# Retention block on one core: when group two's x is quantized for the linear branch, and how the first projection starts

## The reference

```python
xn = _layernorm(x, axis=-1)
# branch 1: retention
q = heads((x @ Wq + bq) * scaling); k = heads(x @ Wk + bk); v = heads(x @ Wv + bv)
ret = einsum('bhid,bhjd->bhij', q, k) * D        # D: causal, decays with distance
ret = ret / clip(abs(ret.sum(-1)), 1.0)
attn = einsum('bhij,bhjd->bhid', ret, v)
g = group norm of attn per head, times gn_w, plus gn_b
out1 = (silu(x @ Wg + bg) * g) @ Wo + bo
# branch 2: linear layer on values rounded to a 4-bit grid in blocks of 16
xq, xs, _ = quantize_nvfp4(x2d, x_tensor_scale)
wq, ws, _ = quantize_nvfp4(weight)
out2 = einsum('mbk,nbk->mn', xq * xs, wq * ws) * output_scale + bias
x = x + out1 + out2
```

## Time and profile before

| | |
|---|---|
| median of three runs | 2097.94 us (2096.73 to 2098.29) |
| the profiled execution | 2103.1 us, its span 2101.3 us |
| PE busy | 2025.2 us, 96% of the span |
| DVE busy | 1643.7 us, 78% |
| ACT / POOL busy | 692.0 us / 888.0 us |
| mean granted TensorE clock | 0.991 of 2.4 GHz |
| DMA | 297.95 MB, mean 142 GB/s |

### The profile page before, as it was taken

One profiled execution on the slowest core, in us unless ns is written; L12 is line 12 of the kernel. 1 busy time (PEld: TensorE's weight loads), 2 busy tenths in 40 slices (PEclk: granted clock), 3 DMA queues, 4 the chain that ended last, 5 costly groups with the idle time before them and its releaser, 6 DMA issues.

```text
span 2101.3 us, 53238 instructions
## 1 busy us (share of the span) xinstructions
PE 2025.2 (96%) x18894; PEld 1118.2 (53%) x18894; DVE 1643.7 (78%) x4375; ACT 692.0 (33%) x1359; POOL 888.0 (42%) x634
## 2 busy tenths in 40 slices
PE   4998989999999999999999999999999999999999
PEld 2444455555555555555555555555555555555544
DVE  7899898889989887777766778777777777777832
ACT  5656532222323232232333233233223233323310
POOL 1233333324333325555434555544554554455530
PEclk8999999999999999999999999999999999999999
DMA  8878643343543434444343355344445435435543
GB/s 309 281 254 283 221 141 101 110 119 101 141 130 109 130 98 118 130 140 122 103 132 115 114 145 141 101 124 125 108 128 142 132 96 140 109 107 145 153 157 116
DMA packets 268714, 297.95 MB, mean 142 GB/s; under 512 B 204224, under 2 KB 204352, under 8 KB 268352
## 3 DMA queue, kind: packets, MB, share of 16 engines
q1 hardware_dynamic: 268624, 296.78, 47.1%
HBM read 205.23 MB, written 41.42 MB: 117 GB/s over the span
## 4 chain that ended last, share of the span: by engine, by line
PE 58%; DVE 33%; issue 5%; DMA 2%; ACT 1%; DVEq 0%; POOL 0%; SPq 0%; POOLq 0%
PE mm L1494 27%; PE mm L1511 9%; PE mm L1422 6%; PE tp L1422 6%; PE mm L1431 3%; DVE state L1239 2%; DVE xa L1032 2%; DVE xa L1031 2%; PE four L1569 2%; DVE xa L1039 2%; DVE gst L1253 2%; PE four L1582 2%; DVE xa L1038 2%; DVE xm L1034 1%; DVE probs L1012 1%
## 5 line engine op out<-in xcount | busy, mean ns | idle before, releaser
L1494 PE MATMUL mm<-xnT,wring 128*128 128x512 f16 x4800 | 1076.6, 382 | 20.0 <-ACT kT L815 9.4
L1494 PEld LDWEIGHTS mm<-xnT,wring 128*128 128x128 f16 x4800 | 462.9, 98 | 562.5 <-issue 24.8
L1511 PE MATMUL mm<-wring,xnT 128*128 128x256 f16 x2688 | 302.8, 273 | 2.4 <-DVE res L1371 2.0
L877 ACT ACTIVATE work<-four,gs 128x64 f32<-128x64 f32 x512 | 158.1, 414 | 399.2 <-DVE gs L1266 399.2
L1511 PEld LDWEIGHTS mm<-wring,xnT 128*128 128x128 f16 x2688 | 261.3, 98 | 47.7 <-DVE res L1371 11.2
L643 POOL TENSOR_TENSOR yT<-gn,gate 128x512 f32 (+1 forms) x64 | 89.6, 1400 | 368.0 <-ACT gn L888 244.9
L1422 PE MATMUL mm<-wo,yT 128*128 128x512 f16 x960 | 215.8, 382 | 2.8 <-POOL yT L648 2.2
L1253 DVE BATCH_NORM_STATS2 gst<-four 128x6 f32<-128x64 f32 x512 | 73.5, 217 | 152.2 <-PE four L1582 151.3
L620 POOL TENSOR_TENSOR qparts<-qT,qparts 128x512 f16<-128x512 f32 x64 | 78.3, 1223 | 254.6 <-ACT qT L815 254.6
L656 POOL TENSOR_TENSOR nparts<-work,nparts 128x512 f16<-128x512 f32 x41 | 47.4, 1156 | 265.1 <-ACT nparts L863 265.1
L1422 PEld LDWEIGHTS mm<-wo,yT 128*128 (+1 forms) x960 | 91.3, 98 | 112.2 <-issue 3.4
(11 more groups left out here) (209 smaller groups left out, 2970.1 us busy)
## 6 DMA issues: line engine op xcount, KB each, us to landing
wring<-parts SPq DMA_DIRECT2D x252, 512.0 KB, 4.2
xt<-in_x SPq DMA_DIRECT2D x34, 512.0 KB, 4.6
out<-res SPq DMA_DIRECT2D x32, 512.0 KB, 3.0
parts<-wo SPq DMA_DIRECT2D x28, 512.0 KB, 5.8
res<-in_x SPq DMA_DIRECT2D x28, 512.0 KB, 3.6
ftile<-in_w_f SPq DMA_DIRECT2D x12, 512.0 KB, 4.9
parts<-wring SPq DMA_DIRECT2D x8, 512.0 KB, 6.9
probs<-in_x SPq DMA_DIRECT2D x5, 512.0 KB, 4.9
```

Of the source, the lines that this page charges most:

```text
L877: last = nc.scalar.activation(work[:, c * P + h * HD:c * P + (h + 1) * HD], ao[h][:, c * VW:c * VW + HD], ACT.Identity, bias=gs[:, 1, g:g ...
L1494: last = MM(mm[n % 2][:], wring[:, slot, wj, k, :], xnT[:, parity, xj, k, :], start=(j == 0), stop=(j == 3 * KT - 1))
L1511: last = MM(out[:, c], xnT[:, parity, xj, k, tokens], wring[:, 1::2, wj, k, :], start=(n == 0), stop=(n == 3 * KT - 1))
```

## The change

It has three parts.

**Quantization moved.** In group one VectorE no longer quantizes. SP stores the normalised rows to a DRAM tensor `xn1` (`keep_xn`), as eight units of 128x512, and the transposes of `xq` and the 1 MB copy to `xq1` are gone. In the eight bodies of groups four and five (the first two of MIDDLE) VectorE does one unit each with 16 instructions in three places: `unit_scales` behind `states(0)`, `unit_grid` behind `mask_scores(1)`, `unit_round` behind the first `emit_linear`. SP adds four DMAs in such a body: the load of the unit, its transpose within SBUF, the store to `xq1`, and in front of this a wait for the transpose, all ahead of `move_n(1)` and of the next body's loads.

**First projection in three passes.** `project_first` does the eight hi·hi matmuls when `hi_done` 1 is there, then hi·lo of x, then lo·hi when `lo_done` 1 is there. The banks that the first transposes of x use are permuted, so that mm0 and mm1 come free early.

**ScalarE's and GpSimd's order at the start.** The evacuation of mm0 comes before `split_hi` of slices 4 and 5, that of mm1 before slices 6 and 7. GpSimd's bias addition waits for `lo_done` 5.

```diff
-        x_banks = [four[:, 2], four[:, 3], four[:, 0], four[:, 1], tp[0], tp[1], mm[0], mm[1]]
+        x_banks = [four[:, 2], mm[0], mm[1], four[:, 3], four[:, 0], four[:, 1], tp[0], tp[1]]
...
+def takes_unit(phase, group):
+
+    return phase == MIDDLE and group < 3 + UNITS // CH
...
+                def keep_xn():
+
+                    w("xn_ready", 1)
+                    sp.dma_start(a["xn1"][2 * i:2 * i + 2].rearrange("h p e -> p h e"),
+                                 xt[:].rearrange("p (h e) -> p h e", h=2)).then_inc(s["xn_kept"], 16)
+
+                def load_unit():
+
+                    w("u_ready", 0)
+                    sp.dma_start(ftile[:, 0:GROUP], a["xn1"][ds(i, 1)].rearrange("a p e -> p (a e)"))\
+                      .then_inc(s["u_loaded"], 16)
+
+                def turn_unit():
+
+                    w("u_ready", 1)
+                    sp.sem_inc(sp_turn, 1)
+                    sp.dma_start(xqf[:, GROUP:].rearrange("p (k t) -> p k t", t=P), xqf[:, 0:GROUP], transpose=True)\
+                      .then_inc(s["u_turned"], 16)
+
+                def keep_unit():
+
+                    w("u_turned", 1)
+                    sp.dma_start(a["xq1"][:, ds(i * GROUP, GROUP)], xqf[:, GROUP:]).then_inc(s["u_kept"], 16)
...
                     load_slice(0, 1)
+                    keep_xn()
                     load_fs(F_TILES[i][0])
...
-                    w("xq_ready", 1)
-                    move_x()
+                    w("xn_kept", 1)
                     load_x(1)
...
+                if takes_unit(phase, group):
+                    load_unit()
                 load_slice(0, 0)
...
+                if takes_unit(phase, group):
+                    turn_unit()
                 move_x()
+                if takes_unit(phase, group):
+                    keep_unit()
                 move_n(1)
...
-                if phase == SECOND:
-                    sp.wait_ge(s["xq_moved"], at("xq_moved", SECOND, 0, 0))
-                    sp.dma_start(a["xq1"], xqT[:, 1].rearrange("p c k t -> p (c k t)")).then_inc(xq1_kept, 16)
...
             pool.wait_ge(bias_in, 16 * 2)
+            pool.wait_ge(lo_done, HK + 1)
...
             split_hi(0, range(0, 4))
             square(0, range(4, SLICES))
-            split_hi(0, range(4, SLICES))
...
                 evacuate(0, 0)
+                if i == 0:
+                    split_hi(0, range(4, 6))
                 evacuate(0, 1)
+                if i == 0:
+                    split_hi(0, range(6, SLICES))
...
+                def unit_scales():
+
+                    w("u_loaded", 1)
+                    quantize_scales(ftile[:, 0:GROUP], x_ts, x_r6, late_qs)
+                    w("u_turned", 0)
+
+                def unit_grid():
+                    find_grid(ftile[:, 0:GROUP], late_qs[:, 4, :])
+
+                def unit_round():
+                    round_to_grid(xqf[:, 0:GROUP], late_qs[:, 3, :]).then_inc(s["u_ready"], 1)
...
                     layernorm(xt[:])
-                    w("xn_ready", 1)
-                    quantize_scales(xt, x_ts, x_r6)
-                    w("xq_moved", 0)
-                    quantize_half(xt, 0)
-                    if i:
-                        quantize_half(xt, 1)
                     mask_scores(0)
-                    if i == 0:
-                        quantize_half(xt, 1)
...
                 states(0)
+                if takes_unit(phase, group):
+                    late_part(unit_scales)
                 group_norm(0)
                 mask_scores(1)
                 if phase in QUANTIZE:
                     f_half(0)
+                if takes_unit(phase, group):
+                    late_part(unit_grid)
                 states(1)
                 emit_half(w, 0, "mm0", 5)
                 if phase == MIDDLE:
                     emit_linear(w, 0, "mm1", 5, "mm0", 5)
+                    if takes_unit(phase, group):
+                        late_part(unit_round)
...
+                def project_first():
+
+                    pe.wait_ge(s["xnT_ready"], CH)
+                    pe.wait_ge(s["xhi_ready"], 2 * CH)
+                    pe.wait_ge(hi_done, 1)
+                    for wj, xj in ((0, 0), (0, 1), (1, 0)):
+                        if xj:
+                            pe.wait_ge(s["xnT_ready"], 2 * CH)
+                        if wj:
+                            pe.wait_ge(lo_done, 1)
+                        for k in range(KT):
+                            last = MM(mm[0][:], wring[:, 0, wj, k, :], xnT[:, 0, xj, k, :],
+                                      start=(k + xj + wj == 0), stop=(wj == 1 and k == KT - 1))
+                    last.then_inc(s["mm0_full"], 1)
```

60 lines of the change are left out of this document (42 added, 18 removed).

## The result

The changed kernel takes 2091.42 us in the median of eight executions (2086.01 to 2092.78), the kernel before 2098.11 (2093.90 to 2101.34, eight): a ratio of 0.9965, interval 0.9954 to 0.9977. That is 6.7 us faster, where 19.1 were forecast; 2091.4 lies 1.4 us above the range. The direction was right, the size was not.

A forecast was written before the change was run, and what follows sets the result against it. VectorE's quantization was taken to delay TensorE in group one, TensorE's own work to bound from group four. 6.7 + 3.9 + 4.1 + 5.9 - 1.5 = 19.1 us off the 2097.9 median gave 2079 us, range 2071 to 2090.

The forecast's parts named there:

- 1.7 us of slow clock: Group one's first body: third projection was to lose its 2.41 us wait and 1.7 us of slow clock.
- DMA included: Group one: 1.5 us taken back for one more VectorE wait on a weight tile, DMA share 0.93 in 55 us.
- Part 1, the first body: Start and first body of group one: earlier first projection and VectorE chain, gain 6.7 us (ends 3.5 and 8.8).
- 3 to 4 us for that slice: First body: the reloaded slice that ScalarE's last square of the second batch needs comes 3 to 4 us sooner.
- Part 2, bodies two to four: Group one: masks no longer wait behind quantization, state increments follow the projection; gains 3.9, 4.1 and 5.9 us.
- the rival that had the rings hold group one: DMA rings hold group one: gain only 8 to 12 us, time 2088 us, chance 0.2.
- Part 3, the units: Groups four and five: eight bodies with VectorE's 16 added instructions and SP's DMAs, costed at 0.
- 10.4 us of VectorE's waits: Groups four and five: VectorE's three waits for TensorE per body, 2.75, 3.61 and 4.07 us, taken to cover the units.
- the slack of the masks: Groups four and five: masks behind group norm have 2.8 us until TensorE needs them.
- if GpSimd stretches all of them: Groups four and five: with all unit instructions stretched, 11 us against 10.4 of waits, costing 0.6 us a body.
- My own sign of being wrong: Forecast is wrong if TensorE idles in bodies with a unit; it was to stay at 99.8% in groups four and five.
- The rival that was to come out slower: Groups four and five: SP's wait for its own transpose delays move_n(1) and weights; 2103 us, chance 0.05.

The follow-up runs named there:

- no_units: Changed kernel without loading, computing or storing units; xq1 filled with group three's values by one DMA: 2084.12 us, ratio 0.9937 to the kernel before.
- the second profile of before: Kernel before, unchanged, run and traced once more: median 2099.43 us, profiled execution 2099.24 us at a clock of 0.993.
- units_dma_only: Changed kernel keeping all four DMAs of a unit, VectorE's 16 instructions replaced by one copy of two columns: 2086.17 us, ratio 0.9934 to the kernel before.
- start_only: Kernel before with only the changed kernel's start (three passes, evacuation order, held-back bias addition, permuted banks), quantization left in group one: 2096.57 us, ratio 0.9992.
- units_early: Changed kernel with unit_round directly behind unit_grid, both ahead of the second states: 2088.86 us, ratio 0.9949 to the kernel before.
- the repetition: Changed kernel, word for word, run again beside the kernel before: 2090.72 us, ratio 0.9967.

## Why the prediction was wrong

**The sum was made on one execution, and fitted it partly by luck.** I wrote that the 19.1 us come off the profiled execution and subtracted them from the median. `no_units`, the changed kernel without the part that I costed at nothing, has a span of 2080.6, 20.7 under the 2101.3 of before; my 19.1 was 1.6 off. But its terms miss in both directions: the first body gave 4.3 us less than I took (2.4 for 6.7), and the rest of group one and the first body of group two 4.2 more (16.6 for 12.4, DMA included).

The terms also held stretches at 1.2 GHz of one execution as if they were the kernel's: the 8.08 of the earlier trace rows, "1.7 us of slow clock" of the third projection, the 2.00 of the earlier trace rows, the 6.45 of the earlier trace rows. Against the second profile of before the trace of `no_units` is 16.8 ahead, and where the changed code meets such stretches itself (`units_dma_only`) it loses up to 4 us to them. In medians the change without units gives 13.5 us (2097.65 to 2084.12), not 19.1. The profiled executions account for the distance between 20.7 and 13.5: that of before stood 5.4 us over its median, at a clock of 0.991 where the mean of 26 executions is 0.994, and that of `no_units` 1.8 under its own, at 0.998 where three of the five have 0.996. I had noted that the profiled execution stood 5.2 us over the median and drew nothing from it, and I took for granted that the changed kernel would run without any.

**Part 1, the first body: mis-sized.** I took 6.7 us. The first pass came at 24.77 (forecast 25.0), the three passes ended at 30.66 (32.5 to 33), the layer norm started at 43.32 (42.4 to 43.4): the start is as I described it, and the lead at the first scores 9.2. The step that failed is "3 to 4 us for that slice": ScalarE's last square came 0.8 us earlier than in the earlier trace rows, and TensorE, which waits for it, met a lower clock behind the wait, so the second body began with 2.4 us in the profiles. Without the store of xn (`start_only`) the square came 2.4 us earlier and the second body began with 5.3. In medians the runs show 1.1 us for this part alone and 0.3 on top of the move. I had seen the full queue and the store of xn ahead of the reload, and then followed VectorE's rows and not the slice's.

**Part 2, bodies two to four: right.** Leads grew by 4.4, 3.1 and 6.1 us where I had 3.9, 4.1 and 5.9. Body lengths of 55, an undisturbed projection at the fourth body, and masks beside TensorE's projection are there. Against the second profile of before they are 4.5, 2.7 and 4.4: the fourth body's 6.1 held 1.6 us of lower clock that the other execution has not, and the 5.9 with it. The 3.0 us more at group two's second body I did not have; 1.3 of them are the first profile's lower clock too, since against the second it is 1.7.

**DMA: not the bound.** A share of 0.90 in the third body against my 0.93; the rival that had the rings hold group one named the time nearest to the measured 2091.4, 2088, by a cause that the bodies refute, since bodies two and three gave 7.5 us together.

**Part 3, the units: costed at 0, measured 6.6 us** (5.5 in the traces). This is the larger of the two errors that the medians show. I compared 10.4 us of VectorE's waits with the units' sum, and checked the slack of the masks. The sum was 8.9 us even with a rounding of 4.1, it fitted, and the group norms behind it start on time. The step that failed is that work inside VectorE's waits costs nothing: I had not followed the chain group norm, last output add, value projection, which has no slack, nor asked what VectorE's rounding does to GpSimd. It holds GpSimd back by 0.4 us, and GpSimd then holds a step of the group norm. That VectorE's instructions are the price is shown by `units_dma_only`; the way by GpSimd is read from the traces of all eight bodies, and `units_early` agrees with it in size. My condition "if GpSimd stretches all of them" came to 0.6 us a body, near the 0.7 measured, but by a sum of waits that was not reached, and I gave it no chance of its own. My own sign of being wrong, TensorE idle in bodies with a unit, came: 98.84 busy of 100 us against 99.81. The rival that was to come out slower looked at SP's queue, which cost nothing: its DMAs alone are free. The Trainium skill (SBUF — State Buffer, section "SBUF: two separate sides") says that a VectorE instruction with two SBUF inputs and a GpSimd one that reads SBUF exclude each other for a whole instruction; the trace agrees, 1.59 and 1.76 us where GpSimd's operations overlap, and 0.69 for the instruction between them, at 933.87, when GpSimd is idle. I used that page for the start and not for the units.

In medians: of the 19.1 forecast, 5.6 are missing without units, for the clock and the first body, which the runs don't part further, and 6.6 are the units' price. That leaves 6.9, which is the repetition's own difference; the first measurement was 6.7.

## What to carry to other kernels

Look at the mean clock of the profiled execution before making a sum on it: price each stretch behind a wait at the undisturbed length, and put what the lower clock adds into the range, for both kernels; where another wait follows in the same body, a stretch of lower clock may cost nothing. Work put into an engine's waits is free only if the chain behind each wait has slack, so follow it until another engine waits. Ask also what the new work does to a neighbour that it slows and is slowed by, since the neighbour's delay can come back in that chain. An edit that lengthens a hardware loop's body can move another loop's code to a place where each pass stalls; look for "issue" idle time at the first instruction of a pass.

## What the runs showed of the hardware

Executions of one kernel have the same waits to some tenths of a us up to their first difference in clock, yet the granted clock behind them differs: 1.00 in four windows of one trace, 0.62 to 0.81 in those of another that runs the same instructions. Three of these stretches cost nothing in the end, since shorter waits gave their time back within the body, and the fourth cost 2.8 us. Over 26 executions of before the time fell by about 1.6 us for each 0.001 of mean clock, in the other sets of 11 to 15 by 1.2 to 2.0.

A VectorE instruction and a GpSimd operation that overlap stretch each other: 128x512 with two inputs takes 0.69 us alone and 1.59 and 1.76 beside GpSimd, GpSimd's operation 1.27 and 1.71, and even a step on 128x8 takes up to 1.16 us and ends with GpSimd's operation.

A loop of VectorE can stall for 4.5 us (2.8 to 5.0 seen) at the head of each pass, with packets in an instruction queue, when the code in front of it grows by some dozens of instructions. The stalled group costs 15 to 27 us, more than the stalls, since TensorE waits up to 6.5 us for late masks and runs at a clock of 0.50 behind that. What the code memory's size or layout is, no run here tells.
